# Cross-attention and FFN in one kernel: another order of scores and values, x and the FFN's weights transposed by VectorE instead of TensorE

## The chip, the cores and the metric

The kernel runs on one core of a Trainium2 chip. The time is the device time of one execution in microseconds (us). Engines are named as in the profile: PE is TensorE, PEld its weight loads, DVE VectorE, ACT ScalarE, POOL GpSimd, SP SyncE, whose queue SPq issues all transfers of this kernel.

## The reference, cut to what matters

```python
B, S, D, H, DH = 16, 64, 512, 32, 128
def xattn(hidden_q, hidden_kv, mask, position_bias, Wq, Wk, Wv, Wo):
    q = (hidden_q @ Wq).reshape(b, lq, h, dh)
    k = (hidden_kv @ Wk).reshape(b, lk, h, dh)
    v = (hidden_kv @ Wv).reshape(b, lk, h, dh)
    score = einsum('bqhd,bkhd->bhqk', q, k) * scale + position_bias      # masked keys: -inf
    probs = softmax(score, axis=-1)
    return einsum('bhqk,bkhd->bqhd', probs, v).reshape(b, lq, h * dh) @ Wo
def ffn(x, base_W, base_b, router_W, router_b, A, B, expert_map):
    base_out = einsum('btd,od->bto', x, base_W) + base_b
    probs = softmax(einsum('btd,nd->btn', x, router_W) + router_b, axis=-1)     # 15 outputs
    topk_p, topk_i = top_k(probs, 8)
    w = weights of the 8 experts, through expert_map
    h = einsum('btd,erd->bter', x, A)
    return base_out + einsum('bter,eor->bto', h * w[..., None], B) * 2.0
x = x + xattn(layernorm(x), ctx, mask, bias, Wq, Wk, Wv, Wo)
x = x + ffn(layernorm(x), ...)
```

## The kernel before, in words

There are 1024 tokens, eight tiles of 128. Every large product is done in three passes over values split into a high and a low part (`product`, six matmuls of 512 columns for one contraction of 256): ScalarE rounds to the high part, VectorE subtracts to get the low one. The projections of V, K and Q run as blocks, 16 each, in Strassen's form with seven products (`times(n, p)`, p from 1 to 7); their sums of weights are made by GpSimd (`sums_of_b`), their halves are combined by ScalarE (`copy_p1`, `copy_u`, `copy_v`, `copy_c12`) and VectorE (`make_c11`, `make_c21`, `make_c22`). V and K are stored to memory and read back by head pairs. The orders of all engines are written out by hand, each engine runs its own list, and SP's list issues the transfers in order.

While K's blocks run (n from 16 to 30), x is normalised for the attention: `moments_of_x` and `normalise` on VectorE, `rstd_of` on GpSimd, then `turn_pair(j)`, j from 4 to 7: TensorE transposes two tiles of x with eight 128 x 128 transposes in every third block, and ScalarE and VectorE split what lands in PSUM (`first_high`, `rows_out`, `last_high`, `sums_of_a`). Q's blocks need this from block 31 on.

Then come the stages of head pairs, i from 0 to 13 in the loop and the last pairs by hand. In stage i TensorE computes the scores of pair i + 1 (`scores(h + 2)`, `scores(h + 3)`), the values of pair i (`times_v(h)`, `times_v(h + 1)`), a block of Q (products 1, 2, 6, 7, then 5, 3, 4) and between those the eight tiles of pair i's Wo product (`times_wo(i, t)`). In the same stage VectorE reads the scores (`biased`), takes the maximum (`largest`), splits outputs (`o_low`) and Q's weights (`lower_of`), adds the Wo tiles to y (`add_tile(i, t)`), weights P (`weights`) and transposes it in blocks of 32 x 32 (`turn_blocks`). P goes to memory and comes back in the order that the value product wants (`store_p`, `load_p`); GpSimd adds the mask to the bias (`add_mask`). ScalarE does the exponentials in halves (`exp(h, half)`), the outputs' high parts (`o_high`) and the roundings. Its list in a stage begins `exp(h + 2, 0)`, `o_high(h, 0)`, `o_high(h, 1)`, `o_high(h + 1, 0)`, `copy_p1(n)`, `o_high(h + 1, 1)`, `exp(h + 2, 1)`, `higher_of(w, 0)`, `exp(h + 3, 0)`, `copy_u(n)`, `exp(h + 3, 1)`, `higher_of(w, 1)`; that of VectorE begins `biased(h + 2)`, `largest(h + 2)`, `biased(h + 3)`, `largest(h + 3)`, the four `o_low` with `make_c11(n)` among them, `lower_of(w, 0)`, `lower_of(w, 1)`, `add_tile(i, 0)`. `times_wo(i, t)` with t of 2 or more waits for `add_tile(i, t - 2)`, since there are two banks (pY).

SP's list in a stage: `load_k(i + 2)` once the scores are done, eight bias transfers, Wq, `load_v(i + 1)` once the values are done, in some stages the FFN's small inputs, then `store_p` and `load_p` of the two heads, then Wo.

The FFN's weights are loaded as they lie, transposed by TensorE in the last stages (`ffn_weights`, 28 transposes) and split from PSUM (`split_ffn`). At the end the second layer norm, the router and the FFN's products run tile by tile.

## Time and profile before

| | us |
|---|---|
| median of 3 runs | 779.62 (775.87 to 779.64) |
| the profiled execution | 777.37 |
| its span, first to last instruction | 775.5 |
| TensorE busy | 766.0 (99%) |
| VectorE busy | 541.8 (70%) |
| ScalarE busy | 384.8 (50%) |
| GpSimd busy | 196.6 (25%) |

The span is what lies between the first and the last instruction of the profiled execution. Busy times are sums over the span; a matmul's end is modelled, so a busy TensorE says only that nothing stopped it for long. Starts in a timeline are in us from the start of the span.

### The profile page before, as it was taken

What the parts mean: (1) busy time and instruction counts of PE and PEld (TensorE: products, weight loads), DVE (VectorE), ACT (ScalarE), POOL (GpSimd) and SP (SyncE); (2) the same over time, 40 slices, a digit from 0 to 9 for tenths busy, and PEclk for the clock granted to TensorE, in tenths of its full rate; (3) what the DMA queues carried; (4) which work ended last, traced back from release to release, by engine and by line L of the source; (5) the groups of instructions that cost most, each with busy time, mean ns of one, the idle gap of its engine ahead of it and who ended that gap; (6) DMA issues with size and microseconds to landing.
All of it is one profiled execution on the core that took longest, in us unless ns stands there. A gap on an engine that the chain in (4) does not pass through costs nothing.

```text
span 775.5 us, 16682 instructions
## 1 busy us (share of the span) xinstructions
PE 766.0 (99%) x6272; PEld 639.1 (82%) x6272; DVE 541.8 (70%) x979; ACT 384.8 (50%) x1110; POOL 196.6 (25%) x203
## 2 busy tenths in 40 slices
PE   9999999999999999999999999999999999999998
PEld 7888888888888888887888888888888888888886
DVE  5874626257677676578778877887678767867974
ACT  5662526245555464475654465435543565426510
POOL 0224041014424433323132312232122313010300
PEclk9999999999999999999999999999999999999999
DMA  6536673244565456577766777556756666541002
GB/s 231 203 123 217 220 244 137 109 140 160 163 190 164 164 163 187 167 235 217 229 181 209 226 208 208 170 176 205 201 165 197 201 188 196 154 148 57 1 15 95
DMA packets 128236, 133.05 MB, mean 172 GB/s; under 512 B 46479, under 2 KB 93583, under 8 KB 128158
## 3 DMA queue, kind: packets, MB, share of 16 engines
q1 hardware_dynamic: 128158, 132.00, 54.3%
q8 instruction: 50, 0.82, 0.4%
q14 instruction: 28, 0.23, 0.1%
HBM read 88.98 MB, written 42.99 MB: 170 GB/s over the span
## 4 chain that ended last, share of the span: by engine, by line
PE 94%; DVE 3%; issue 1%; ACT 1%; DMA 0%; ACTq 0%
PE pY L1452 43%; PE pP L1452 40%; PE pY L1613 4%; PE pO L1649 2%; PE pT_ L1649 1%; PE pO L1452 1%; DVE y L1167 1%; ACT pr L798 1%; PE pS L1649 1%; DVE st L1018 1%; PE pO L1501 0%; PE pS L1501 0%; DVE wk_lo L948 0%; PE pY L1528 0%; DVE wo_lo L948 0%
## 5 line engine op out<-in xcount | busy, mean ns | idle before, releaser
L798 ACT ACTIVATE pr<-pr,mx 128x64 f32<-128x64 f32 x256 | 86.2, 343 | 68.0 <-DVE mx L1187 68.0
L1452 PE MATMUL pY<-wo_hi,oT_hi 128*128 128x512 f32 x248 | 97.3, 392 | 0.3 <-DVE y L1167 0.2
L1452 PE MATMUL pY<-wo_lo,oT_hi 128*128 128x512 f32 x248 | 96.6, 389 | 0.0
L1452 PE MATMUL pY<-wo_hi,oT_lo 128*128 128x512 f32 x248 | 96.5, 389 | 0.0
L1167 DVE TENSOR_TENSOR y<-y,pY 128x512 f32<-128x512 f32 x124 | 83.9, 676 | 15.2 <-PE pY L1452 14.1
L690 ACT CAST wk_hi<-twk 128x256 fp32r<-128x256 f32 x128 | 50.7, 408 | 65.2 <-PE pP L1452 53.4
L948 DVE TENSOR_TENSOR wk_lo<-wk_raw,wk_hi 128x256 fp32r<-128x256 f32 x96 | 48.5, 506 | 46.5 <-ACT wk_hi L690 45.1
L1452 PE MATMUL pP<-xo_hi,wk_hi 128*128 128x512 f32 x196 | 77.9, 398 | 0.0
L1452 PE MATMUL pP<-xo_lo,wk_hi 128*128 128x512 f32 x196 | 76.4, 390 | 0.0
L1452 PE MATMUL pP<-xo_hi,wk_lo 128*128 128x512 f32 x196 | 76.4, 390 | 0.0
L623 POOL TENSOR_TENSOR bias<-bias,madd 128x512 f32<-128x512 f32 x32 | 41.3, 1306 | 137.6 <-DMA bias<-in_fside_Bx32xSxS 137.5
L948 DVE TENSOR_TENSOR wk_lo<-twk,wk_hi 128x256 fp32r<-128x256 f32 x128 | 54.5, 438 | 23.5 <-ACT wk_hi L690 23.5
L606 POOL TENSOR_TENSOR twk<-wk_raw 128x256 f32<-128x256 f32 x32 | 25.1, 784 | 168.3 <-DVE wk_lo L948 135.3
L1452 PEld LDWEIGHTS pY<-wo_hi,oT_hi 128*128 128x128 f32 x248 | 46.5, 188 | 11.7 <-DVE y L1167 1.5
L1452 PEld LDWEIGHTS pY<-wo_lo,oT_hi 128*128 128x128 f32 x248 | 46.6, 188 | 9.8
L1452 PEld LDWEIGHTS pY<-wo_hi,oT_lo 128*128 128x128 f32 x248 | 46.6, 188 | 9.3
L798 ACT ACTIVATION_READ_ACCUMULATOR pr<-pr,mx 128x1 f32 x256 | 49.5, 193 | 0.0
L1452 PE MATMUL pP<-co_hi,wk_hi 128*128 128x512 f32 x126 | 49.3, 392 | 0.0
L1452 PE MATMUL pP<-co_lo,wk_hi 128*128 128x512 f32 x126 | 49.1, 389 | 0.0
L1452 PE MATMUL pP<-co_hi,wk_lo 128*128 128x512 f32 x126 | 49.0, 389 | 0.0
L1452 PE MATMUL pY<-wv_hi,co_hi 128*128 128x512 f32 x112 | 43.8, 391 | 0.1
L1452 PE MATMUL pY<-wv_lo,co_hi 128*128 128x512 f32 x112 | 43.6, 389 | 0.0
(283 smaller groups left out, 1862.2 us busy)
## 6 DMA issues: line engine op xcount, KB each, us to landing
v_hbm<-stage SPq DMA_DIRECT2D x64, 256.0 KB, 2.1
k_hbm<-stage SPq DMA_DIRECT2D x64, 256.0 KB, 3.7
k<-k_hbm SPq DMA_DIRECT2D x16, 1024.0 KB, 6.4
v<-v_hbm SPq DMA_DIRECT2D x16, 1024.0 KB, 7.2
wk_raw<-in_L_xattn_Wk SPq DMA_DIRECT2D x16, 512.0 KB, 4.6
wo_raw<-in_L_xattn_Wo SPq DMA_DIRECT2D x16, 512.0 KB, 3.7
bias<-in_fside_Bx32xSxS SPq DMA_DIRECT2D x128, 64.0 KB, 3.6
wk_raw<-in_L_xattn_Wq SPq DMA_DIRECT2D x16, 512.0 KB, 4.6
```

The costliest lines, as they stand in the source:

```text
L606: nc.gpsimd.tensor_tensor(tw[:, 0, :, :], raw_block(w, 1, 1), raw_block(w, 0, 1), ALU.subtract).then_inc(tw_made, 1)
L623: nc.gpsimd.tensor_tensor(b[:, :, :], b[:, :, :], madd[:, :, :], ALU.add).then_inc(bias_made, 1)
L690: nc.scalar.copy(w_part(w, 0)[:, slot, :, :], w_source(w, slot)).then_inc(w_hi[slot], 1)
L798: nc.scalar.activation(pr[s][:, b, :], pr[s][:, b, :], ACT.Exp, bias=mx[:, s, b:b + 1], accum_out=sm[:, s, b:b + 1]).then_inc(exp_made, 1)
L948: nc.vector.tensor_tensor(dst, src, hi.bitcast(F32), ALU.subtract).then_inc(done, 1)
L1018: nc.vector.bn_stats(st[:, n % NX, :], y[:, t, :]).then_inc(ln_step, 1)
L1167: nc.vector.tensor_tensor(y[:, t, :], y[:, t, :], src[:, :], ALU.add).then_inc(y_added, 1)
L1452: mm = nc.tensor.matmul(bank_, a, b, start=first and n == 0, stop=last and n == len(terms) - 1, skip_group_check=read_between)
L1613: mm = nc.tensor.matmul(pY[s][64 * half:64 * half + 64, blk * S:(blk + 1) * S], q[:, s, b * S:(b + 1) * S], k[:, s, b * S:(b + 1) * S], st ...
L1649: mm = nc.tensor.matmul(o, (v if h >= 2 else v0)[rows, t, s * DH + 64 * d:s * DH + 64 * d + 64], p, start=True, stop=True)
```

## The change

Four things. (1) In the loop of head pairs TensorE's order becomes values of the first head, scores of both heads, values of the second head; in stage 0 a product of the Q block goes between. The lists of ScalarE and VectorE in the loop stay. (2) x for the attention: VectorE transposes the normalised tiles in blocks of 32 x 32 (`xb`), SP stores them and loads them back so that whole tiles come out transposed (`x_out`, `x_back`), and ScalarE and VectorE split from SBUF instead of PSUM; the steps of x begin a block earlier. (3) The FFN's weights are loaded in pieces such that a transposition of 32 x 32 blocks in place, by VectorE, gives the transposed weights; `ffn_weights` goes. The transfers of A, the router and base_W move behind Wo's load of stages 2 and 3. (4) In the last stages the order on all engines is changed, the last pair's outputs get buffers of their own (`oT_last`), pair 14's Wo products use four banks (`pQ`), and some waits are split.

```diff
+    bw_d = base_W.rearrange("(b k) (c g j) -> g k c b j", k=32, g=4, j=32)
+    a_d = A_in.rearrange("e r d -> (e r) d").rearrange("(b k) (c g j) -> g k c b j", k=32, g=4, j=32)
+    r_d = router_W.rearrange("n (c g j) -> g n c j", g=4, j=32)
+    b_d = B_in.rearrange("(g f) (b k) r -> g f k b r", f=2, k=32)
...
+            def x_out(j):
+                for i in range(2):
+                    sp.wait_ge(xb_made, 2 * j + i + 1)
+                    sp.dma_start(x_hbm[2 * j + i], xb[:, i, :, :].rearrange("p a n -> p (a n)")).then_inc(put_x[i], 16)
+            def x_back(j):
+                if j >= 1:
+                    sp.wait_ge(sum_step, 4 * (4 + j))
+                    sp.wait_ge(a01_lo, 4 + j)
+                    sp.wait_ge(a6_lo, 4 + j)
+                for i, dst in enumerate((first_x, low[1])):
+                    sp.wait_ge(put_x[i], 16 * (j + 1))
+                    blocks = x_hbm[2 * j + i].rearrange("(t k) (a n) -> a k t n", t=4, a=4)
+                    for a in range(4):
+                        sp.dma_start(dst[32 * a:32 * a + 32, :, :], blocks[a]).then_inc(ld_xt[i], 16)
...
                     load_wk(n - 10)
+                if 17 <= n < 29 and n % 3 == 2:
+                    x_out((n - 17) // 3)
                 if n != Q0:
                     store(n, 0, c11_made)
                 if 0 < n:
                     store(n - 1, 2, c21_made)
+                if 17 <= n < 29 and n % 3 == 2:
+                    x_back((n - 17) // 3)
...
-                if i == 2:
-                    sp.dma_start(a_raw[:, :], a_d).then_inc(ld_a, 16)
-                    sp.dma_start(r_raw[:, :], router_W).then_inc(ld_a, 16)
-                if i == 3:
-                    sp.dma_start(bw_raw[:, :, :], bw_d).then_inc(ld_ffn, 16)
                 if i == 4:
-                    for o in range(DC):
-                        sp.dma_start(b_raw[:, o, :].rearrange("p (e r) -> p e r", e=E), b_d[:, o]
-                                     ).then_inc(ld_ffn, 16)
+                    for g in range(4):
+                        for f in range(2):
+                            sp.dma_start(b_raw[32 * g:32 * g + 32, :].rearrange("k (b f r) -> k f b r", f=2, r=R)[:, f],
+                                         b_d[g, f]).then_inc(ld_ffn, 16)
                 h = 2 * i + 2
                 if by_blocks(h):
                     store_p(h)
                     store_p(h + 1)
                     load_p(h)
                     load_p(h + 1)
                 if i + 2 < NP:
                     sp.wait_ge(wo_l, i + 2)
                     load_wo(i + 2)
+                if i == 2:
+                    sp.wait_ge(ar_clear, 1)
+                    for g in range(4):
+                        rows = slice(32 * g, 32 * g + 32)
+                        for c in range(DC):
+                            sp.dma_start(ar_raw[rows, c, 0:ER].rearrange("k (b j) -> k b j", j=32), a_d[g][:, c]
+                                         ).then_inc(ld_a, 16)
+                        sp.dma_start(ar_raw[32 * g:32 * g + NR, :, ER:ER + 32], r_d[g]).then_inc(ld_a, 16)
+                if i == 3:
+                    for g in range(4):
+                        for c in range(DC):
+                            sp.dma_start(bw_raw[32 * g:32 * g + 32, c, :].rearrange("k (b j) -> k b j", j=32),
+                                         bw_d[g][:, c]).then_inc(ld_ffn, 16)
...
 (ScalarE, K blocks)
                     first_high(j)
-                    rows_out(j)
                     last_high(j)
...
 (VectorE, normalise)
+                for i in range(2):
+                    m = 2 * n + i
+                    dve.wait_ge(xn_made, m + 1)
+                    if n >= 1:
+                        dve.wait_ge(put_x[i], 16 * n)
+                    nc.vector.transpose(xb[:, i, :, :].rearrange("p g (c q) -> p c g q", c=DC),
+                                        xn[:, i, :].rearrange("p (c g q) -> p c g q", c=DC, g=4)).then_inc(xb_made, 1)
...
 (VectorE, loop of pairs, after add_tile(i, 7))
+                if 6 <= i < 8 + DC:
+                    dve.wait_ge(ld_a, 320)
+                    dve.wait_ge(ld_ffn, 384)
+                    raw = {6: ar_raw[:, :, :].rearrange("p c n -> p (c n)"), 7: b_raw[:, :]}.get(i)
+                    raw = bw_raw[:, i - 8, :] if raw is None else raw
+                    nc.vector.transpose(raw, raw).then_inc(fw_turned, 1)
...
 (VectorE, last stages)
+            o_low(h, 0)
+            o_low(h, 1)
             biased(h + 2)
             largest(h + 2)
-            o_low(h, 0)
-            o_low(h, 1)
             o_low(h + 1, 0)
             o_low(h + 1, 1)
             biased(h + 3)
             largest(h + 3)
-            split_ffn(0)
             add_tile(i, 0)
-            split_ffn(1)
             add_tile(i, 1)
             add_tile(i, 2)
             invert(i + 1)
             weights(h + 2)
+            weights(h + 3)
             add_tile(i, 3)
-            weights(h + 3)
+            split_ffn(0)
+            add_tile(i, 4)
+            split_ffn(1)
+            add_tile(i, 5)
+            lower_wo(NP - 1)
             split_ffn(2)
-            add_tile(i, 4)
+            add_tile(i, 6)
             split_ffn(3)
-            add_tile(i, 5)
-            add_tile(i, 6)
-            add_tile(i, 7)
-            lower_wo(NP - 1)
-            split_ffn(4)
             o_low(h + 2, 0)
             o_low(h + 2, 1)
             o_low(h + 3, 0)
             o_low(h + 3, 1)
+            add_tile(i, 7)
+            split_ffn(4)
             split_ffn(5)
-            split_ffn(6)
...
 (TensorE, K blocks)
-                if prep_at(n) is not None:
-                    turn_pair(prep_at(n))
...
 (TensorE, loop of pairs)
                 if i == 0:
                     turn_p(h)
                     turn_p(h + 1)
-                scores(h + 2)
-                scores(h + 3)
-                times_v(h)
+                    scores(h + 2)
+                    scores(h + 3)
+                    times_v(h)
+                    times(n, 2)
+                else:
+                    times_v(h)
+                    scores(h + 2)
+                    scores(h + 3)
                 times_v(h + 1)
-                for p in (1, 2, 6, 7) if i else (2, 6, 7):
+                for p in (1, 2, 6, 7) if i else (6, 7):
                     times(n, p)
...
 (TensorE, last stages)
+            times_v(h)
             scores(h + 2)
-            times_v(h)
             times_v(h + 1)
             scores(h + 3)
-            ffn_weights(0)
-            ffn_weights(1)
-            for t in range(4):
-                times_wo(i, t)
-            ffn_weights(2)
-            ffn_weights(3)
-            for t in range(4, NT):
+            for t in range(3):
+                times_wo(i, t, heads=(0,))
+            for t in range(3):
+                times_wo(i, t, heads=(1,))
+            for t in range(3, 6):
                 times_wo(i, t)
             turn_p(h + 2)
             turn_p(h + 3)
-            ffn_weights(4)
+            times_wo(i, 6)
             times_v(h + 2)
+            times_wo(i, 7)
             times_v(h + 3)
-            ffn_weights(5)
-            ffn_weights(6)
...
             pe.wait_ge(o_lo, 2 * H - 2)
-            pe.wait_ge(y_added, last_pair * NT)
             for t in range(4):
+                if t < 2:
+                    pe.wait_ge(y_added, last_pair * NT - 1 + t)
                 times_wo(last_pair, t, heads=(0,))
```

## Rows read from the trace of the kernel before

**Rows 1.** The page, busy time of each engine, its share of the span, instructions.

```profile
PE 766.0 (99%) x6272; PEld 639.1 (82%) x6272; DVE 541.8 (70%) x979; ACT 384.8 (50%) x1110; POOL 196.6 (25%) x203
```

**Rows 2.** Busy time by stretch, a K block without and one with x's transposes.

```profile
core 0: us, PE busy (x) PEld busy (x) DVE busy (x) ACT busy (x) POOL busy (x), PEclk, DMA share, GB/s
158.43:167.94 9.51, 9.51 (x43) 7.87 (x43) 5.22 (x12) 4.58 (x11) 2.32 (x3) 1.00 0.32 113
177.47:187.87 10.40, 10.40 (x51) 8.71 (x51) 6.91 (x15) 5.59 (x13) 4.82 (x6) 1.00 0.54 163
```

**Rows 3.** Busy time by stretch: pairs 1 to 13, then pairs 6 and 10.

```profile
368.84:695.48 326.64, 322.77 (x3669) 270.27 (x3670) 250.42 (x431) 164.03 (x617) 77.86 (x71) 1.00 0.65 193
494.50:519.22 24.72, 24.72 (x284) 20.68 (x286) 19.53 (x33) 12.76 (x48) 6.57 (x7) 1.00 0.60 190
595.30:619.98 24.68, 24.68 (x285) 20.74 (x286) 19.22 (x33) 12.76 (x48) 6.63 (x7) 1.00 0.66 196
```

**Rows 4.** The list of waits: us in total, times, longest.

```profile
PE pT_ L1649 <- issue: 3.9, 5, 1.0
```

**Rows 5.** Busy time by stretch, four stretches of the FFN weights' transposes, and their sum.

```profile
699.60:701.28 1.68, 1.68 (x13) 1.09 (x9) 1.68 (x4) 1.68 (x12) 0.00 (x0) 1.00 0.76 210
...
sum 4.12, PE 4.12 PEld 3.10 DVE 4.12 ACT 3.48 POOL 0.00; mean PE 1.03 PEld 0.77 DVE 1.03 ACT 0.87 POOL 0.00
```

**Rows 6.** Busy time by stretch, from the last loop stage to pair 15's Wo.

```profile
695.48:717.87 22.39, 22.29 (x404) 18.90 (x405) 18.01 (x30) 13.51 (x49) 0.00 (x0) 1.00 0.17 55
```

**Rows 7.** Timeline of PE, from values to scores: start, us, engine line op.

```profile
698.37 0.22 PE L1649 MATMUL pS<-pT,v 64*64 64x64 f32 x1
698.51 1.15 PE L1613 MATMUL pY<-k,q 128*64 128x64 f32 x32
```

**Rows 8.** Timeline of DVE in pair 6; in brackets the idle time before.

```profile
495.63 0.69 DVE L1178 SCALAR_TENSOR_TENSOR pr<-pY,bias 128x512 f32<-128x512 f32 x1 [0.40 <-PE pY L1613]
...
506.34 0.94 DVE L948 TENSOR_TENSOR wk_lo<-wk_raw,wk_hi 128x256 fp32r<-128x256 f32 x1 [3.02 <-ACT wk_hi L690]
507.20 0.67 DVE L1167 TENSOR_TENSOR y<-y,pY 128x512 f32<-128x512 f32 x1
```

**Rows 9.** Timeline of DVE in pair 10.

```profile
596.43 0.69 DVE L1178 SCALAR_TENSOR_TENSOR pr<-pY,bias 128x512 f32<-128x512 f32 x1 [0.41 <-PE pY L1613]
...
607.14 0.43 DVE L948 TENSOR_TENSOR wk_lo<-wk_raw,wk_hi 128x256 fp32r<-128x256 f32 x1 [3.02 <-ACT wk_hi L690]
607.48 0.68 DVE L1167 TENSOR_TENSOR y<-y,pY 128x512 f32<-128x512 f32 x1
...
609.77 0.71 DVE L1210 STREAM_TRANSPOSE pb<-pr 128x512 f32<-128x512 f32 x1
```

**Rows 10.** Timeline of ACT in pair 6.

```profile
497.07 0.35 ACT L798 ACTIVATE pr<-pr,mx 128x64 f32<-128x64 f32 x1 [4.87 <-DVE mx L1187]
...
500.17 0.59 ACT L663 COPY c_s<-pP 128x512 f32<-128x512 f32 x1 [0.23 <-PE pP L1452]
```

**Rows 11.** Timeline of POOL in pair 6.

```profile
505.70 1.29 POOL L623 TENSOR_TENSOR bias<-bias,madd 128x512 f32<-128x512 f32 x1 [0.52 <-DMA bias<-in_fside_Bx32xSxS]
```

**Rows 12.** Timeline of PE in pair 6, Wo's tile 2.

```profile
508.14 0.40 PE L1452 MATMUL pY<-wo_hi,oT_hi 128*128 128x512 f32 x1
```

**Rows 13.** Timeline of SP's queue in pair 4, which begins at 443.9.

```profile
445.97 0.38 SPq L449 DMA_DIRECT2D k<-k_hbm  x1
446.40 6.66 SPq L442 DMA_DIRECT2D bias<-in_fside_Bx32xSxS  x8
...
453.75 0.51 SPq L452 DMA_DIRECT2D v<-v_hbm  x1
454.30 6.90 SPq L566 DMA_DIRECT2D b_raw<-in_L_ffn_B  x4
461.25 1.48 SPq L457 DMA_DIRECT2D p_hbm<-pb  x2
```

**Rows 14.** Timeline of SP's queue in pair 10.

```profile
613.48 3.64 SPq L465 DMA_DIRECT2D pT<-p_hbm  x8
617.34 0.40 SPq L446 DMA_DIRECT2D wo_raw<-in_L_xattn_Wo  x1
```

More of the change, by code:

```diff
@@ L351, in raw_block, with first_of, second_of, like @@
             return raw[:, 2 * r:2 * r + 2, c * width:(c + 1) * width]
+        def first_of(j):
+            if j < 4:
+                return first_turn(j)[:, :].rearrange("p (c t) -> p c t", c=DC)
+            return first_x[:, :, :].rearrange("p t (c q) -> p c t q", c=DC)
+        def second_of(j):
+            if j < 4:
+                return second_turn(j)[:, :].rearrange("p (c t) -> p c t", c=DC)
+            return low[1][:, :, :].rearrange("p t (c q) -> p c t q", c=DC)
+        def like(j, a):
+            return a if j < 4 else a.rearrange("p c (t q) -> p c t q", t=4)
+        def outputs(pair):
+            return oT_last if pair == NP - 1 else oT
+        def y_tile(pair, t):
+            return {NP - 1: pL, NP - 2: pQ}.get(pair, pY + pY)[t % 4]
         def tw_of(w):
@@ L692, in first_high @@
             def first_high(j):
-                act.wait_ge(turned, FIRST_TURN[j] + 1)
-                nc.scalar.copy(a_part(j, 0)[:, 0:2, :, tile_cols(j)],
-                               first_turn(j)[:, :].rearrange("p (k c t) -> p k c t", k=2, c=2)).then_inc(a01_hi, 1)
+                if j < 4:
+                    act.wait_ge(turned, FIRST_TURN[j] + 1)
+                else:
+                    act.wait_ge(ld_xt[0], 64 * (j - 3))
+                nc.scalar.copy(like(j, a01_of(j, 0)), first_of(j)).then_inc(a01_hi, 1)
             def rows_out(j):
@@ L706, in last_high @@
             def last_high(j):
-                cols = tile_cols(j)
-                act.wait_ge(turned, SECOND_TURN[j] + 1)
-                nc.scalar.copy(a_part(j, 0)[:, 6, :, cols],
-                               second_turn(j)[:, 2 * P:4 * P].rearrange("p (c t) -> p c t", c=2)).then_inc(a6_hi, 1)
+                if j < 4:
+                    act.wait_ge(turned, SECOND_TURN[j] + 1)
+                else:
+                    act.wait_ge(ld_xt[1], 64 * (j - 3))
+                nc.scalar.copy(like(j, a_part(j, 0)[:, 6, :, tile_cols(j)]), second_of(j)[:, 2:4]).then_inc(a6_hi, 1)
             def sums_high(j):
@@ L811, in o_high @@
                 act.wait_ge(o_full, 2 * h + n + 1)
-                if s == 0 and n == 0 and i >= 1:
+                if i == NP - 1:
+                    act.wait_ge(prod, DONE[NBLK - 1, 4])
+                    act.wait_ge(s_full, H)
+                elif s == 0 and n == 0 and i >= 1:
                     act.wait_ge(y_full, NT * i)
-                nc.scalar.copy(of_parity(oT[0], s, n), pO_of[s][n][:, :].rearrange("p (t q) -> p t q", q=S)
+                nc.scalar.copy(of_parity(outputs(i)[0], s, n), pO_of[s][n][:, :].rearrange("p (t q) -> p t q", q=S)
                                ).then_inc(o_hi, 1)
@@ L904, in _ @@
             exp(h + 2, 1)
-            split_ffn(0)
             exp(h + 3, 0)
-            split_ffn(1)
             exp(h + 3, 1)
-            split_ffn(2)
-            split_ffn(3)
+            for n in range(4):
+                split_ffn(n)
             wo_high(NP - 1)
+            split_ffn(4)
             turned_p(h + 2)
             turned_p(h + 3)
-            split_ffn(4)
+            split_ffn(5)
+            split_ffn(6)
             o_high(h + 2, 0)
@@ L1165, in add_tile @@
                 dve.wait_ge(y_full, pair * NT + (t + 1))
-                src = pL[t % 4] if pair == last_pair else pY[t % 2]
+                src = y_tile(pair, t)
                 nc.vector.tensor_tensor(y[:, t, :], y[:, t, :], src[:, :], ALU.add).then_inc(y_added, 1)
@@ L1403, in _ @@
             for i in range(NT + 3):
+                if i == NT:
+                    split_ffn(6)
                 if i < NT:
@@ L1654, in times_wo @@
             def times_wo(pair, t, heads=(0, 1)):
-                if pair < last_pair:
+                if pair < last_pair - 1:
                     if t == 0:
@@ L1664, in times_wo @@
                         pe.wait_ge(y_added, pair * NT + t - 1)
-                dst = pL[t % 4] if pair == last_pair else pY[t % 2]
+                elif pair == last_pair - 1 and heads[0] == 0:
+                    if t == 0:
+                        pe.wait_ge(wo_l, pair + 1)
+                        pe.wait_ge(o_lo, 4 * pair + 2)
+                        pe.wait_ge(c12_made, NBLK)
+                        pe.wait_ge(c21_made, NBLK)
+                    if t in (2, 3):
+                        pe.wait_ge(s_read, 2 * pair + 1 + t)
+                    elif t >= 4:
+                        pe.wait_ge(y_added, pair * NT + t - 3)
+                if pair == last_pair - 1 and heads[-1] == 1 and t == 0:
+                    pe.wait_ge(o_lo, 4 * (pair + 1))
+                dst = y_tile(pair, t)
                 cols = slice(t * P, (t + 1) * P)
-                o, w = oT, wo[pair % 2]
+                o, w = outputs(pair), wo[pair % 2]
                 mm = product(dst[:, :], [((o[0][:, i, cols], o[1][:, i, cols]), (w[0][:, i, :], w[1][:, i, :]))
```

152 lines of the change are left out of this document (63 added, 89 removed).

## Prediction

> **What bounds the kernel now.** I read the page first. TensorE is busy for 766.0 of 775.5 us [rows 1] and its granted clock is full in all forty slices, so at first sight whatever leaves TensorE is won. The second view is busy time by stretch. A block of the K stage takes 9.51 us, all of it TensorE, and the same block with a turned pair of x tiles 10.40 [rows 2]. In the stage of head pairs, thirteen pairs take 326.64 us, 25.13 each; a pair that nothing disturbs takes 24.68, and TensorE idles 3.87 us in all thirteen [rows 3]. The list of waits names that idle time: five times about 1 us inside the value products, put down to "issue", so to no engine and no transfer that the profile shows [rows 4]. They fall where 128 small matmuls follow 64 others without a break. The third view, the timeline of each engine in one pair, shows how near the other engines are to deciding: VectorE is busy 19.2 to 19.5 us of a pair [rows 3], and its first addition of a Wo tile ends 0.27 us before TensorE starts the product that waits for it [rows 8, 12]. So this is a TensorE kernel with little slack behind it, and what decides is whether the new order still keeps that slack.
>
> **x through VectorE.** The change takes 32 transposes of x off TensorE: four blocks at 10.40 - 9.51 = 0.89 us [rows 2], 3.6 us gained. VectorE gets two block transposes for each pair of tiles, 0.71 us each by the like one [rows 9], 1.4 us in a block where it is busy 5.22 of 9.51 us [rows 2]; ScalarE loses a copy. SyncE issues two stores and eight loads for each pair, behind which two stores of K wait a few us; their buffers are used again two blocks, 19 us, later. The x pieces are needed first in block 31, the last come back in block 27. I cost this at nothing; without that cover it would be 1.4 us in each of four blocks, 5.7 us.
>
> **The FFN weights.** The four stretches of TensorE with their transposes sum to 4.12 us [rows 5], all of which leave. In their place VectorE has six transposes in pairs 6 to 11, 0.71 us each, behind its last addition of the pair. There it waits 0.40 us for the scores now [rows 8], and 1.15 us more by the new order (below), so they cost nothing; if the order gave no more room, 6 x 0.3 = 1.9 us.
>
> But the 4.12 us are not all won. In this part VectorE is busy 18.01 of 22.39 us [rows 6]. The new last pair starts its second Wo tile only after VectorE's addition of tile 7, which now stands behind four output splits. VectorE's list up to that point has 22 instructions of 0.69 us (eight output splits, two reads and two maxima of the scores, eight additions, two weightings), 15.2 us, and some 2.3 for four weight splits, 1.2 for Wo's and 0.45 for the reciprocals: 19.1 us, from about 1.9 us after the start, plus some 0.5 us of waiting for the exponentials and 0.5 for the last values: 21.9 to 22.1. From there seven half products of 0.68 us end at 26.8, against 27.9 now. I take -1.2 us; the bounds are -3.6 (TensorE alone decides: 4.12 less some 0.5 for switches) and 0.
>
> **Values, scores, values.** A switch of TensorE from value products to scores costs 0.14 us start to start, where value matmuls are 0.01 apart [rows 7]; the new order has one more switch in each pair. Bare TensorE time is thus 24.68 + 0.14 = 24.82. The issue stalls may go, because 128 small matmuls no longer follow the scores in one run.
>
> What the order moves is the chain behind the scores. TensorE now runs one head's values first, half of a 2.0 us stretch, and the switch: the scores come 1.15 us later in the pair. ScalarE's and VectorE's lists stay as they are: ScalarE takes the exponentials of the new scores before it rounds the outputs, and is idle for 4.87 us waiting for them [rows 10]. Behind them stand the outputs, the first product's copy, more exponentials, a weight's rounding; then VectorE's split of that weight and the addition of Wo tile 0, for which TensorE waits before tile 2. From VectorE's first read of the scores (495.63) to tile 2 on TensorE (508.14) it is 12.51 us [rows 8, 12]. In a pair where GpSimd does not overlap, read to addition is 608.16 - 596.43 = 11.73 [rows 9], with the same 0.27 to TensorE 12.00.
>
> After the change the read starts 1.13 + 1.15 = 2.28 us into the pair. ScalarE gives back the 0.23 us that it idles before the copy [rows 10]. Tile 2 so starts at 2.28 + 12.00 - 0.23 = 14.05 at best, and at 2.28 + 12.51 = 14.79 where GpSimd is in the way, against 13.85 at which TensorE could. From tile 2 to the next pair it is 519.22 - 508.14 = 11.08 [rows 3, 12]. So the period is 25.13 to 25.87, against 25.13 on average now: 0 to +8.9 us in twelve pairs. I take 25.6, because GpSimd's second mask addition follows the bias load, which follows the scores: it ends at 506.99 [rows 11], 12.49 into the pair, and would end at 13.64, while VectorE's split would start 506.34 - 494.50 + 0.92 = 12.76 in. They overlap in every pair then, and overlapped the split takes 0.94 us instead of 0.43 [rows 8, 9]. That is +5.6 us. The issue stalls lie inside this wait from then on; at worst five of them stick out by 0.45, 2.3 us. Pairs 0 and 13 get the switch and a little waiting: +0.6.
>
> The Trainium skill (SBUF — State Buffer, Who interferes with whom) says that a VectorE instruction with two SBUF inputs is blocked outright by a GpSimd instruction that reads SBUF, for that whole instruction. The trace agrees: the split ended 0.29 us after GpSimd did. By that rule alone the period is that of the later engine, about 25.6; without it 25.1.
>
> **The weights' transfers.** They go in pieces now, since VectorE transposes blocks of 32 x 32: 20 transfers for A and router instead of 2, behind pair 2's last load, 16 for base_W instead of 1 behind pair 3's, 8 for B instead of 4 ahead of pair 4's P. All are on SyncE's one queue, in order, with the next pair's k, bias, v and the way of P through memory. One such issue costs 3.64/8 = 0.46 (P) to 6.66/8 = 0.83 us (bias) [rows 13, 14].
>
> SyncE ends a pair's list 2.2 us before the pair ends (wo at 617.74, [rows 3, 14]). So base_W's 16 issues (7.3 to 13.3 us) last until 5 to 11 us into pair 4, where k is issued at 2.1 now. From k to v it is 453.75 + 0.51 - 445.97 = 8.3, B takes 6.9, and from P's store to the home-coming of the first head's last quarter (four of eight loads and about 2 us to land) some 6.5 [rows 13]. P is there 26.7 to 33 us into the pair, and the next pair now begins with it, without 2 us of scores as cover. Against 25.6 that is 1 to 7 us late. Behind A's transfers pair 3 is 0 to 4 us late (its P is made at 610.48, 15.2 into the pair [rows 9], 16.4 then). What is queued behind it is everything: values, scores and the rest of TensorE. I take +4 us; bounds 0 (it lands in time) and 11.
>
> A rule speaks against this change: the Trainium skill (DMA: Bandwidth & Descriptors, Specifications) wants 512 B or more in a piece for line rate, and base_W now comes in pieces of 128 B. By the issue times alone the stall is the above.
>
> **Sum**: -3.6 - 1.2 + 5.6 + 0.6 + 4 = +5.4 us. The profiled execution took 777.37 us (span 775.5 and 1.9 around it), so 782.8; the median of the runs shown is 779.62, 2.2 above it, so I say 784.
>
> **Rivals.** (1) It gets faster: the chain behind the scores has more slack than I read. It decides at tile 2 of each pair: where VectorE's first addition is done 13.7 us into the pair or sooner, the period is 24.82 and the loop gains 12 x 0.31 = 3.7 us instead of losing 5.6. With the end at -3.6, x at -3.6, and P in time, it is 769. For it: the stalls of [rows 4] are real and the order breaks up their run; TensorE has nothing else to wait for in [rows 3]. Against: ScalarE's list is not reordered, and 14.05 is its best by the rows. (2) No change: the chain binds as I say, but P lands in time, or the pair is nearer 25.2: -3.6 - 1.2 + 4 + 0.6, 777 to 782. For it: bounds of the issue time that reach down to no stall in pair 3 and 1 us in pair 4. (3) The pieces are slow in themselves, not only to issue: B's 4096 pieces held SyncE 6.90 us [rows 13]; base_W's 8192 at that rate take 14 us and A's 2300 another 4, so pair 4 gets P another 5 us later: 789 to 793. This is the skill's rule above, as a mechanism of this queue. For it: B's transfers, issued while v was under way, took up to three times their shortest time. Against: that may have been v.
>
> **Chances**: forecast 0.45 (781 to 788), rival 1 0.15, rival 2 0.26, rival 3 0.14. About 0.5%, 3.9 us, is what a measurement of this kernel can tell from no change. Slower by more: 0.59; within: 0.25; faster: 0.16. The range that leaves out some 2 in 10 is 774 to 793; it cuts off rival 1's core.
>
> **What would show it.** The K blocks with x take 9.5 us, as their neighbours. Pairs 1 to 12 take 25.1 to 25.9 us, TensorE waits at Wo tile 2 for VectorE's addition, and the five issue stalls are gone or inside. One long wait stands ahead of the value products of pair 5 (a shorter one at pair 4), with P's load as its end, and SyncE issues k in pair 4 at 6 us or later. The last part is about 1 us shorter, with a wait for tile 7's addition. I am wrong if pairs take 24.8 us, if no wait for P shows, or if VectorE's transposes push a K block past 9.6 us.

## The result, and the profile after

The changed kernel takes 790.96 us (median of 4 runs, 789.90 to 792.16), the kernel before 779.63 beside it: the ratio is 1.0177, 95% interval 1.0157 to 1.0196, so slower by 1.8%. The forecast was slower, 784.0, at most 793. The direction held, the size did not: +0.6% was said. (The kernel before had one run of 1092 us in that set, which the ratio leaves out; the quotient of the two medians is 1.0145, while the ratio on record fits the 776.7 to 777.4 us that the kernel before takes beside the experiments.) The profiled execution took 790.88 us, its span 789.1, 13.6 more than before.

Busy times of the page, to be read against [rows 1], and the granted clock in forty slices:

```profile
PE 768.4 (97%) x6212; PEld 635.0 (80%) x6212; DVE 551.2 (70%) x994; ACT 382.2 (48%) x1106; POOL 196.6 (25%) x203
...
PEclk9999999999999999999999998999999999999999
```

TensorE has 60 instructions fewer, yet is busy 2.4 us longer, and it idles more: 20.7 us of the span instead of 9.5. One slice has a lower clock. So some work runs slower, and there are waits. Busy time by stretch says where (columns as in [rows 2]): a K block in which VectorE now transposes x, one in which TensorE formerly did, the block that has x's last pair; pairs 1 and 2; 3; 4; 5; 6; 6 to 13; and from the last pairs to the end:

```profile
173.86:183.38 9.52, 9.52 (x43) 7.89 (x42) 6.97 (x15) 4.79 (x11) 3.37 (x5) 1.00 0.62 214
183.38:192.91 9.53, 9.53 (x44) 7.75 (x42) 7.64 (x17) 6.42 (x14) 1.71 (x3) 1.00 0.76 227
269.29:280.05 10.76, 9.79 (x43) 7.72 (x42) 7.72 (x17) 6.47 (x14) 2.60 (x4) 1.00 0.67 206
367.97:418.93 50.96, 50.57 (x566) 41.51 (x565) 39.01 (x67) 25.31 (x96) 13.11 (x13) 1.00 0.67 194
418.93:448.55 29.62, 25.46 (x283) 20.69 (x283) 21.53 (x43) 12.66 (x48) 7.29 (x7) 1.00 0.56 159
448.55:481.62 33.07, 26.97 (x282) 22.20 (x283) 19.96 (x33) 12.66 (x48) 7.08 (x6) 0.92 0.78 184
481.62:508.55 26.93, 26.93 (x282) 22.82 (x283) 18.67 (x32) 12.67 (x48) 6.03 (x6) 0.91 0.66 191
508.55:533.66 25.11, 25.11 (x283) 20.75 (x282) 18.96 (x33) 12.66 (x48) 6.64 (x7) 1.00 0.62 185
508.55:710.95 202.40, 201.27 (x2258) 166.08 (x2257) 154.90 (x263) 99.15 (x377) 45.08 (x41) 1.00 0.62 183
710.95:789.10 78.15, 73.08 (x681) 61.85 (x680) 57.87 (x151) 28.07 (x76) 6.77 (x16) 1.00 0.13 47
```

Up to pair 1 the kernel gains 0.8 us (367.97 against 368.77); thirteen pairs take 342.98 against 326.64 [rows 3], a loss of 16.3; the rest takes 78.15 against 775.5 - 695.4 = 80.1, a gain of 1.9. Pairs 3 to 5 alone take 89.62. The other ten take 50.96 + 202.40 = 253.36, 25.34 each, so the disturbance of pairs 3 to 5 costs 89.62 - 3 x 25.34 = 13.6 us, as much as the whole difference. The new order costs 13 x (25.34 - 25.13) = 2.7.

The list of PE's waits after the first 20 us:

```profile
PE pO L1738 <- DMA pT<-p_hbm: 9.4, 2, 5.5
PE pY L1551 <- DVE y L1253: 2.8, 4, 1.7
PE pS L1738 <- issue: 1.3, 3, 0.8
PE pY L1551 <- ACT u_s L738: 1.0, 1, 1.0
```

Two waits for P on its way back from memory are the bulk; from start to start they cost 4.0 us (at the end of pair 3) and 5.7 (of pair 4). The third row is the issue stalls, fewer but not gone. The longest wait for VectorE's y, 1.7, lies in the last part.

SP's queue from the end of pair 2 to that of pair 4, beside [rows 13]; pair 3 begins at 418.93, pair 4 at 448.55:

```profile
416.70 0.40 SPq L502 DMA_DIRECT2D wo_raw<-in_L_xattn_Wo  x1
417.14 1.89 SPq L638 DMA_DIRECT2D ar_raw<-in_L_ffn_A  x4
...
429.16 0.86 SPq L640 DMA_DIRECT2D ar_raw<-in_L_ffn_router_W  x1
430.07 0.55 SPq L505 DMA_DIRECT2D k<-k_hbm  x1
...
437.18 0.51 SPq L508 DMA_DIRECT2D v<-v_hbm  x1
437.73 1.25 SPq L513 DMA_DIRECT2D p_hbm<-pb  x2
445.18 3.64 SPq L521 DMA_DIRECT2D pT<-p_hbm  x8
...
449.35 10.31 SPq L644 DMA_DIRECT2D bw_raw<-in_L_ffn_base_W  x16
459.70 0.49 SPq L505 DMA_DIRECT2D k<-k_hbm  x1
...
467.30 8.21 SPq L622 DMA_DIRECT2D b_raw<-in_L_ffn_B  x8
475.56 0.96 SPq L513 DMA_DIRECT2D p_hbm<-pb  x2
478.20 3.64 SPq L521 DMA_DIRECT2D pT<-p_hbm  x8
```

SyncE issues A and the router until 430.02; pair 3's k is asked for 11.1 us into the pair instead of 2.1. The chain of waits says what came of that:

```profile
437.73 7.44 DMA p_hbm<-pb
```

P's store needed 7.44 us from its issue to P's load; in the kernel before it was 464.06 - 461.25 = 2.8 in pair 4 [rows 13] and 4.2 in pair 3. It stands behind k, eight bias transfers, Wq and v, 3072 KB by the page's sizes. The kernel before has the same 3072 KB ahead of the store in every pair; what differs is the distance to v, 0.55 us here. In the fourteen profiles together, twelve stores of P were issued 0.5 to 1.2 us behind v, and they took 7.4 to 7.8 us to land; the 380 that were issued 4.9 us or more behind v took 2.0 to 4.5. In pair 4 the store comes at 475.56, 27.0 us into the pair, behind sixteen issues of base_W (10.31 us) and eight of B (8.21): there it is the issues that last.

### The profile page after: what moved, and what is told of

Read it like the earlier page. It is cut to its first block, busy times and chain, and to the rows that moved or that the text cites. A ratio compares the mean times of both kernels' runs of the same rounds, so it can differ in the third digit from the quotient of the medians.

```text
span 789.1 us, 16665 instructions
## 1 busy us (share of the span) xinstructions
PE 768.4 (97%) x6212; PEld 635.0 (80%) x6212; DVE 551.2 (70%) x994; ACT 382.2 (48%) x1106; POOL 196.6 (25%) x203
## 4 chain that ended last, share of the span: by engine, by line
PE 79%; SPq 7%; DVE 6%; DMA 4%; ACT 2%; issue 2%; ACTq 0%; DVEq 0%
PE pY L1551 36%; PE pP L1551 35%; PE pY L1702 3%; PE pO L1738 2%; SPq L498 1%; PE pT_ L1738 1%; DMA p_hbm<-pb 1%; ACT pr L869 1%; SPq L644 1%; DVE y L1253 1%; DMA wv_raw<-in_L_xattn_Wv 1%; SPq L638 1%; SPq L622 1%; DVE wk_lo L1023 1%; PE pO L1551 1%
## 5 line engine op out<-in xcount | busy, mean ns | idle before, releaser
L1551 PE MATMUL pY<-wo_hi,oT_hi 128*128 128x512 f32 x232 | 91.6, 395 | 1.3 <-DVE y L1253 1.1
L1551 PE MATMUL pY<-wo_hi,oT_lo 128*128 128x512 f32 x232 | 90.6, 390 | 0.0
L1551 PE MATMUL pY<-wo_lo,oT_hi 128*128 128x512 f32 x232 | 90.5, 390 | 0.0
L1253 DVE TENSOR_TENSOR y<-y,pY 128x512 f32<-128x512 f32 x120 | 80.8, 673 | 12.4 <-PE pY L1551 12.4
L1023 DVE TENSOR_TENSOR wk_lo<-wk_raw,wk_hi 128x256 fp32r<-128x256 f32 x96 | 45.1, 477 | 53.1 <-ACT wk_hi L759 52.7
L1023 DVE TENSOR_TENSOR wk_lo<-twk,wk_hi 128x256 fp32r<-128x256 f32 x128 | 59.4, 477 | 20.2 <-ACT wk_hi L759 20.2
L1551 PEld LDWEIGHTS pY<-wo_hi,oT_hi 128*128 128x128 f32 x232 | 43.6, 188 | 13.9 <-DVE y L1253 4.8
L1551 PEld LDWEIGHTS pY<-wo_lo,oT_hi 128*128 128x128 f32 x232 | 43.6, 188 | 9.1
L1551 PEld LDWEIGHTS pY<-wo_hi,oT_lo 128*128 128x128 f32 x232 | 43.6, 188 | 8.5
L1551 PEld LDWEIGHTS pP<-xo_hi,wk_hi 128*128 128x128 f32 x196 | 36.8, 188 | 11.0 <-issue 3.1
```

What stands on the lines that cost most here:

```text
L1023: nc.vector.tensor_tensor(dst, src, hi.bitcast(F32), ALU.subtract).then_inc(done, 1)
L1253: nc.vector.tensor_tensor(y[:, t, :], y[:, t, :], src[:, :], ALU.add).then_inc(y_added, 1)
L1551: mm = nc.tensor.matmul(bank_, a, b, start=first and n == 0, stop=last and n == len(terms) - 1, skip_group_check=read_between)
```

## Experiments

Times are medians beside the kernel before on the same chip (776.7 to 777.4), so the ratios are what compares; the changed kernel's is 1.0177.

**e1_spread.** Behind v in SyncE's list, with the old places taken out:

```diff
+                if 2 <= i < 6:
+                    g = i - 2
...
+                    for c in range(DC):   # ar_raw, slot c, rows of g
...
+                    for f in range(2):    # b_raw, half f, rows of g
...
+                if 6 <= i < 8:
+                    for g in (2 * i - 12, 2 * i - 11):   # bw_raw, four transfers each
```

> The changed kernel, with the FFN's 44 transfers issued elsewhere: seven (five of A and the router, two of B) in each of pairs 2 to 5 and eight of base_W in pairs 6 and 7, all between v's load and P's store, where SyncE's list has some 5 us of waiting. Theory (SyncE's queue makes P late in pairs 3 and 4): both long waits go, 4.0 and 5.7 us, and the slower clock after them with 3.6 us; pairs 3 to 5 take 25.1 to 25.6 us, in all 776 to 779 us. Rival (the small pieces load the DMA engines and P comes late wherever they are issued): waits for P remain in pairs 2 to 7, 784 us or more.

779.25 us, ratio 1.0035 (1.0023 to 1.0048). Pairs 3 to 5, and the kernel from the last pairs to the end:

```profile
417.26:442.38 25.12, 25.12 (x284) 20.74 (x283) 18.96 (x33) 12.66 (x48) 6.54 (x7) 1.00 0.70 202
442.38:467.58 25.20, 25.12 (x283) 20.88 (x282) 19.90 (x42) 12.67 (x48) 6.55 (x7) 1.00 0.68 196
467.58:493.40 25.82, 25.51 (x283) 20.58 (x282) 19.78 (x33) 12.66 (x48) 6.43 (x7) 1.00 0.65 180
697.65:777.30 79.65, 74.63 (x681) 62.97 (x680) 57.88 (x151) 28.08 (x76) 6.77 (x16) 0.98 0.13 46
```

The theory holds: 11 us come back with no change of the work. The time is 0.25 us above the theory's range. What is still lost is 0.5 and 0.8 us of waiting for P at the ends of pairs 6 and 7, where base_W's eight issues behind v took 9.2 us, a stall of 2.1 us in pair 8's values, and 1.5 us in the last part: it takes 79.65 us where the changed kernel has 78.15, since the granted clock falls to 0.50 at 719.96 us, just behind the wait of 1.7 us for tile 7's addition.

**e2_wide.**

```diff
-sp.dma_start(bw_raw[32 * g:32 * g + 32, c, :].rearrange("k (b j) -> k b j", j=32), bw_d[g][:, c])
+sp.dma_start(bw_raw[32 * g:32 * g + 32, c, :], bw_w[32 * g:32 * g + 32, c, :])   # A and B alike
```

> The changed kernel with as many transfers of as many bytes at the same places, but A, base_W and B come in pieces of 512 B, 2 KB and 1 KB instead of 128, 128 and 64 B (so that A, base_W and B are not transposed and the output is another). Theory (the time that SyncE needs for each issue, some 0.45 to 1.0 us whatever the pieces, makes P late): both waits stay within 1.5 us of 4.0 and 5.7 us, 788 to 792 us in all. Rival (small pieces are slow in themselves): the waits shrink by half or more, 784 us or less.

783.88 us, ratio 1.0099 (1.0074 to 1.0123): just inside the rival's range. PE's waits in pairs 3 to 5, and two rows of SP's queue in pair 4 (from 446.14):

```profile
PE pO L1739 <- DMA pT<-p_hbm: 5.1, 2, 4.0
...
462.52 4.34 SPq L625 DMA_DIRECT2D b_raw<-in_L_ffn_B  x8
466.90 0.90 SPq L516 DMA_DIRECT2D p_hbm<-pb  x2
```

The first wait stays (4.1 us start to start), so A's cost is the number of issues, as the theory has it. The second falls from 5.7 to 1.3, with some 0.5 more for the second head: B's eight issues take 4.34 us instead of 8.21, and P's store comes 20.8 us into the pair instead of 27.0. There the rival is right, and it is the third rival of the prediction: small pieces are slow in themselves, above all where they are issued behind v, still under way. Base_W's sixteen issues, behind Wo, took 10.31 us with pieces of 128 B and 8.28 with 2 KB. (These rows are of an execution of 782.02 us with a mean granted clock of 0.998; two of the four had 0.993 and took 785.7 and 787.0, and no trace shows their waits.) The Trainium skill (DMA: Bandwidth & Descriptors, Specifications) wants 512 B or more in a piece for line rate; the rows agree for B, and for A they show no difference in the wait.

**e12_b_late.** `if i == 4:` ahead of B's transfers becomes `if i == 6:`.

> The changed kernel with B's eight transfers moved from pair 4 to the same place in pair 6. Theory (in pair 4 base_W's sixteen issues make k, bias, Wq and v as late as A's twenty did in pair 3, and P's store then queues behind v; B's eight add the rest): the wait ahead of pair 5's values shrinks from 5.7 us to that of pair 4, 3.5 to 4.5 us, and pair 7 waits for P by 0.5 us or so in its place: 787 to 790 us. Rival (B's small pieces alone hold up P in pair 4): the wait ahead of pair 5 falls to 1.5 us or less, 784 to 786 us.

786.57 us, ratio 1.0132 (1.0104 to 1.0160). The wait ahead of pair 5 is 2.9 us, some 0.5 more for the second head, and that of pair 4 stays at 4.1; none appears at pair 7. So of the 5.7 us some 2 to 3 are B's; the rest is base_W's and, with B gone, the store's, which now stands right behind v in pair 4 too:

```profile
465.94 0.51 SPq L508 DMA_DIRECT2D v<-v_hbm  x1
466.49 1.28 SPq L513 DMA_DIRECT2D p_hbm<-pb  x2
474.31 3.65 SPq L521 DMA_DIRECT2D pT<-p_hbm  x8
```

Both theories' waits were off, by 0.6 us and by 1.4 or more; the time is 0.4 below the theory's range, and behind the shorter wait the granted clock stayed at 1.00 in the profiled execution.

**e11_after_old.** The changed kernel with the old order in the loop:

```diff
-                    times_v(h)
                     scores(h + 2)
                     scores(h + 3)
+                    times_v(h)
                 times_v(h + 1)
```

> The changed kernel with one thing undone: in the loop of pairs from 1 on TensorE takes the scores of both heads first again, then the values. Theory (P comes late by SyncE's queue whatever TensorE's order, but the scores, 2.1 us, stand ahead of the values as cover): the waits for P shrink from 4.0 and 5.7 us to about 1.9 and 3.6 (0.5 us either way), the slower clock after them costs less, and pairs without a wait take 24.7 us: 780 to 784 us. Rival (the waits come back in full, because with the scores first k, bias and P of the next pair are asked for as late): 785 us or more.

785.33 us, ratio 1.0106 (1.0082 to 1.0130). The theory falls. PE's waits in pairs 4 and 5:

```profile
PE pO L1738 <- DMA pT<-p_hbm: 7.3, 2, 5.5
PE pT_ L1738 <- DMA pT<-p_hbm: 2.5, 1, 2.5
```

In pair 4 the first head's wait is shorter by 2.0 us, the scores' length, but the second head then waits 2.7 us, which the scores covered in the new order. In pair 5 it is 5.7 again. P comes back when SyncE gets to it: at 481.8 here, at 481.6 in the changed kernel. From 417 to 482 us SyncE's list, with the landing of P's stores, is the bound, and what TensorE does first there is of no account.

**e4_clock.**

```diff
+            def keep_clock(i, count):
+                pe.wait_ge(c12_made, QA + 2 + i)
+                pe.wait_ge(c21_made, QA + 2 + i)
+                for m in range(count):
+                    nc.tensor.matmul(pP[0][:, :], oT[0][:, 0, 0:P], wo[(i - 1) % 2][0][:, 0, :], start=True, stop=True)
...
+                    if i in (4, 5):
+                        keep_clock(i, {4: 16, 5: 22}[i])
                     times_v(h)
```

> The changed kernel; at the start of pairs 4 and 5, ahead of the wait for P, TensorE does 16 and 22 matmuls of 512 columns that nobody reads, 3.6 and 5.0 us, inside the waits of 4.0 and 5.7 us. Theory (after a wait of this length TensorE's granted clock is at half for 3 to 4 us, which costs 1.55 and 2.07 us in the bursts of pairs 4 and 5): the waits for P stay, the bursts take 4.2 us again, 787 to 788 us. Rival (the slow bursts come from transfers or instructions arriving late, not from the clock): the bursts stay slow and the time is 790 to 792 us.

Values and scores at the start of pairs 6, 4 and 5 of the changed kernel, by stretch:

```profile
508.55:512.75 4.20, 4.20 (x194) 4.00 (x193) 2.56 (x4) 0.46 (x3) 0.68 (x1) 1.00 0.24 89
448.55:454.29 5.74, 5.74 (x192) 5.50 (x192) 1.92 (x3) 0.51 (x3) 0.00 (x0) 0.70 0.78 173
481.62:487.90 6.28, 6.28 (x192) 6.03 (x192) 2.27 (x4) 0.89 (x5) 0.00 (x0) 0.62 0.40 118
```

and the starts of pairs 4 and 5 in e4_clock:

```profile
447.20:451.50 4.30, 4.13 (x180) 3.86 (x184) 1.98 (x3) 0.57 (x3) 0.00 (x0) 1.00 0.83 198
480.03:484.50 4.47, 3.65 (x144) 3.38 (x148) 1.55 (x3) 0.73 (x5) 0.00 (x0) 1.00 0.54 164
```

With something to do through the wait TensorE keeps its clock. Without it the same 192 matmuls take 5.74 and 6.28 us instead of 4.20, at a mean granted clock of 0.70 and 0.62; in the 4.35 us from 481.65 it is 0.50, the lower of its two levels, 1.2 of 2.4 GHz. The Trainium skill (TensorE: Matmul & The Clock Gate, What's actually happening) says that an idle TensorE is put to half its clock; the trace agrees for these two waits. But the time is 788.45 us, ratio 1.0154 (1.0138 to 1.0170), just above the theory's range; it is some 2 us less and not 3.6: what pair 4 gains its end gives back, since P comes no earlier (e11 again), and in pair 5 an issue stall of 1.0 takes half.

**e3_spread_old.** e1_spread with the old order (the edit of e11_after_old).

> The kernel with the spread transfers (e1_spread), and in the loop of pairs from 1 on TensorE's old order: scores of both heads, then values of both. Theory (in the new order TensorE waits in nearly every pair for ScalarE's copy of the first product, 0.29 us, and has one more switch of 0.14 us; the old one has only the issue stalls): an undisturbed pair takes 24.7 us again, some four or five issue stalls of about 1 us come back, the mean pair is 25.1 and the time 2 to 4 us below e1_spread, so 773 to 776 us. Rival (the new order pays for itself by taking the issue stalls away): within 1 us of e1_spread or above it.

775.26 us, ratio 0.9976 (0.9962 to 0.9990): 4.0 us below e1_spread and inside the theory's range. By the profiles not all of that is the order: 1.5 us of it is the slower clock in e1_spread's last part, which takes 78.15 us here.

**e5_even_old.** e3_spread_old, with this in place of the sixteen transfers of base_W:

```diff
+                if 6 <= i < 6 + DC:
+                    c = i - 6
+                    for g in range(4):   # bw_raw, slot c, rows of g
```

> e3_spread_old with base_W's sixteen transfers four to a pair in pairs 6 to 9 instead of eight in pairs 6 and 7. In e3_spread_old eight of them took SyncE 9.4 us (pair 7), P came 0.4 us late and pair 8 lost 4.2 us to a stall of 2.5 us inside the values and the slower clock behind it. Theory (too many issues between v and P's store make P late, and a wait or stall of over 2 us also costs clock): pairs 7 and 8 come back to 24.7 to 25.7 us, 3 to 4 us in all: 771 to 773 us where e3_spread_old had 775.3. Rival (that stall is one of the issue stalls, whose places are a matter of the instruction stream alone): pair 8 keeps 2 us or more of stall, 774 to 776 us.

771.99 us, ratio 0.9932 (0.9919 to 0.9945). Pairs 7 and 8 take 24.67 and 25.61; PE waits for P nowhere. The theory's numbers came. Whether its cause did is open: e7_even_new_p1, with the same transfers, has a stall of 2.0 us in pair 9. What the record shows is that the mean granted clock was 1.000 in all five executions here and below that in eight of e3_spread_old's twelve; the other four took 772.3 to 773.5 us, 1 us more than this kernel. The theory's "over 2 us" is no rule: in e1_spread a stall of 2.1 us left the clock at 1.00, and a wait of 1.7 us was followed by 0.50.

**e7_even_new_p1.** e5_even_old's transfers, the new order, and in ScalarE's list:

```diff
                 o_high(h, 0)
                 o_high(h, 1)
-                o_high(h + 1, 0)
                 if i:
                     copy_p1(n)
+                o_high(h + 1, 0)
                 o_high(h + 1, 1)
```

> The transfers as in e5_even_old, TensorE's new order (values, scores, values), and in ScalarE's list of a pair the copy of the first product moves up by one, ahead of the rounding of the third output. Theory (in the new order the 0.29 us inside the Q block's products is the wait for the bank that this copy empties): an undisturbed pair takes 24.82 us instead of 25.11, or up to 24.95 if Wo's tile 2 then waits; the mean pair is 24.9 to 25.1, and the time within 1 us of e5_even_old. Rival (the chain behind the scores binds at Wo's tile 2 anyway): pairs stay at 25.1, the time 2 to 4 us above e5_even_old.

775.23 us, ratio 0.9979 (0.9967 to 0.9992), 3.2 above e5_even_old. An undisturbed pair takes 25.05. TensorE no longer waits for the copy: product 6 begins 7.08 us into pair 6 instead of 7.24. But product 7 now waits for VectorE's `make_c11`, which stands behind an output split that the move made later (done at 8.41, the product begins at 8.56), and smaller delays follow. So the copy was the wait, and the next in line stood just behind it. The rival's time came, though not for its reason: at Wo's tile 2, 14.08 us in, VectorE's addition has been done for 0.4.

**e6_even_old_tail.** e5_even_old, and in VectorE's last list:

```diff
-            split_ffn(2)
             add_tile(i, 6)
-            split_ffn(3)
             o_low(h + 2, 0)
             o_low(h + 2, 1)
+            add_tile(i, 7)
             o_low(h + 3, 0)
             o_low(h + 3, 1)
-            add_tile(i, 7)
+            split_ffn(2)
+            split_ffn(3)
```

> e5_even_old, and in the last stages VectorE's addition of tile 7 stands behind two of the last output splits instead of four, and ahead of two weight splits that stood before it. Theory (TensorE's 1.9 us of idle time ahead of the last pair's second Wo tile is the wait for that addition alone, and nothing else comes late there): 1.2 to 1.9 us below e5_even_old. Rival (VectorE's list is the bound in the last stages, and what is put off is missed later): within 0.5 us of e5_even_old.

771.10 us, ratio 0.9919 (0.9906 to 0.9933), 0.9 below e5_even_old. In the profile the wait is gone and the last part takes 76.70 us instead of 78.12, 1.4 less; the medians show less than the theory's 1.2, within their spread.

**e8_x_later.** In ScalarE's K blocks `copy_u(n)` goes ahead of `last_high(j)`.

> e6_even_old_tail, and in the K blocks ScalarE rounds the second tile of x behind the copy of the sixth product instead of ahead of it. In the changed kernel TensorE idles 1.1 us in block 27 (0.7 to 0.8 in the runs since) for that copy, which stands behind a rounding that waits for x to come back from memory. Theory: the idle time goes and nothing else comes late, 0.6 to 0.9 us below e6_even_old_tail. Rival (the sums of x come late for Q's first block, or the run's own spread covers it): no difference, within 0.5 us.

770.72 us, ratio 0.9916 (0.9899 to 0.9932): no difference that can be told, and no test either, since that idle time was not in e6_even_old_tail's profile to begin with. It came in some executions, 0 to 1.1 us.

**e9_break and e10_before_break.** The break of the small matmuls (192 in a pair, with their weight loads 384 instructions), in e8_x_later and in the kernel before:

```diff
                 times_v(h)
+                if i:
+                    times(n, 1)
                 times_v(h + 1)
-                for p in (1, 2, 6, 7) if i else (2, 6, 7):
+                for p in (2, 6, 7):
```

> e8_x_later, and in the loop of pairs TensorE's run of small matmuls is broken in another way: scores of both heads, values of the first head, the Q block's first product, values of the second head; ScalarE's copy of that product moves up by one. Theory (the issue stalls come from 384 small matmuls in a row asking for instructions faster than they come, and the scores still lead the pair, so no chain is later): the stalls of 0.3 to 1.2 us in five or six pairs go, each pair pays some 0.2 us for two more switches, the mean pair 24.9 instead of 25.05: 1 to 3 us below e8_x_later. Rival (the stalls go elsewhere, or the switches eat the gain): within 1 us of e8_x_later.

> The kernel before, with this other break alone: the Q block's first product between the values of the two heads, and ScalarE's copy of it one place earlier. Theory: the five issue stalls of the kernel before, 4.9 us in all, go; thirteen pairs pay 0.2 us each; 1.5 to 3 us below the kernel before. Rival: no difference, or slower by up to 3 us, because the stalls stay and the switches come on top.

772.55 us, ratio 0.9936 (0.9920 to 0.9953), and 777.43, ratio 1.0002 (0.9993 to 1.0012). Pairs 1 to 13 of the kernel before with the break, and of e8_x_later without it:

```profile
369.27:695.27 326.00, 326.00 (x3667) 269.63 (x3666) 248.58 (x431) 163.70 (x617) 77.69 (x71) 1.00 0.65 193
...
366.27:692.21 325.94, 322.30 (x3668) 270.04 (x3667) 252.86 (x438) 163.74 (x617) 78.17 (x71) 1.00 0.67 192
```

With the break TensorE is busy for all of the 326.00 us: every issue stall of [rows 4] is gone, so they do come from the long run of small matmuls. That instructions come too slowly fits, but is not shown: in the kernel before each of the five stalls ends 1.4 to 1.5 us after a packet of the profile's instruction queue has landed. Each pair takes 25.05 to 25.11 instead of 24.68, and that eats the gain: thirteen pairs take 326.00 us against 326.64 in the kernel before [rows 3], and 325.97 in e9_break against 325.94 in e8_x_later. The rival wins in the kernel before; e9_break's median is 1.8 us above e8_x_later, outside both. In its profile, an execution of 774.5 us, 3.7 us more lie ahead of pair 1, about 3 of them in the first 13 us, where the granted clock rose at 13.1 us instead of 6.1 and no instruction differs. e8_x_later has the lowest median here, 0.8% below the kernel before and 2.6% below the changed one; e6_even_old_tail can't be told from it.

## Why the prediction was wrong

**The weights' transfers, +4 us, is the step that failed.** The mechanism was named as it happened: SyncE's one queue, pairs 3 and 4, k at 6 us or later (11.1), P as the end of the wait, and e1_spread gets it back. Its size was not: 13.6 us, beyond the bound of 11.

Three things were missing. First, the two waits were put at 0 to 4 and 1 to 7 us and then taken at 4 together; they are 4.0 and 5.7. In pair 3 the way of P from its store to TensorE took 448.55 - 437.73 = 10.8 us where the prediction has 6.5, because the store was issued right behind v. That made SyncE's list late: base_W's issues, expected 2.2 us ahead of pair 4, begin 0.8 us into it; and B's took 8.2 us where 6.9 was said. Second, TensorE falls to half clock in waits of that length, which was put at nothing: 1.5 and 2.1 us in the bursts behind them. Third, k, bias and Wq come late too, so VectorE's additions do: TensorE waits 0.5 and 0.8 us more inside pairs 3 and 4.

The measured time lies in the band of the third rival, given 0.14, and that rival was partly true at once with the forecast: by e2_wide some 6 of the 13.6 us come with the small pieces. They were not alternatives. That the scores had been cover for P, as the prediction said, does not hold here: in e11_after_old they stand ahead of the values again, and P lands as late.

**Values, scores, values: +5.6 in the loop.** The sign held; the size is 2.7 by the profile against the kernel before, and 4.0 by e1_spread against e3_spread_old, clock included. The place was wrong. Pair 6, which begins at 508.55, on ScalarE, PE, GpSimd and VectorE:

```profile
515.05 0.60 ACT L732 COPY c_s<-pP 128x512 f32<-128x512 f32 x1
...
515.40 0.39 PE L1551 MATMUL pP<-xo_lo,wk_hi 128*128 128x512 f32 x1
515.79 0.47 PE L1551 MATMUL pP<-xo_hi,wk_hi 128*128 128x512 f32 x1
...
518.80 2.54 POOL L692 TENSOR_TENSOR bias<-bias,madd 128x512 f32<-128x512 f32 x2 [9.57 <-DMA bias<-in_fside_Bx32xSxS]
...
521.23 0.43 DVE L1023 TENSOR_TENSOR wk_lo<-wk_raw,wk_hi 128x256 fp32r<-128x256 f32 x1 [3.02 <-ACT wk_hi L759]
521.57 0.68 DVE L1253 TENSOR_TENSOR y<-y,pY 128x512 f32<-128x512 f32 x1
...
522.69 0.39 PE L1551 MATMUL pY<-wo_hi,oT_hi 128*128 128x512 f32 x1
```

Undisturbed, the matmul at 515.40 is followed by the next one 0.23 us later; here it is 0.39. So 7.1 us into the pair TensorE waits for ScalarE's copy of the first product, whose bank product 6 needs (e7_even_new_p1); the chain was followed to Wo's tile 2, past a nearer consumer. At tile 2 (14.14 us in, the "at best" was 14.05) VectorE's addition has been done for 0.4 us: it ends 13.7 us in, as the first rival asked, and yet the pair does not take that rival's 24.82. (The 13.85 at which TensorE could start tile 2 does not fit the prediction's own 24.82 - 11.08 = 13.74; no term hangs on it.) GpSimd's mask additions end 12.8 us in, back to back and not at 13.6, and VectorE's split, which begins 12.7 in, takes 0.43: they hardly meet, so the 25.6 that was taken on that ground should have been the lower end, 25.13; the undisturbed pair is 25.11. Issue stalls were not gone: 0.3 to 1.0 us in pairs 1, 8, 9 and 12.

**x: -3.6.** The blocks fell from 10.40 to 9.53 as said. But block 27 took 10.76, with TensorE waiting 1.0 us for a ScalarE copy behind x's return, which was costed at nothing; pair 0 took 0.7 more, for which with pair 13 0.6 was said; and 0.65 us was lost in the first 40 us, where no changed instruction runs. So 0.8 was left at pair 1. That is one execution: in the nine other profiles with the same instructions up to there pair 1 begins at 365.90 to 367.87 us, 0.9 to 2.9 ahead of the kernel before.

**FFN weights and the last part: -1.2.** It was -1.9, inside the bounds, with the predicted wait for tile 7's addition (1.7 us). e6_even_old_tail shows that the wait was one of order, not of VectorE's load.

The sum: -0.8 + 2.7 + 13.6 - 1.9 = 13.6 us, against +5.4. The first rival failed. What left TensorE is worth 5 us all the same, as the forecast's two negative terms say, once the transfers are spread and the old order is kept (e5_even_old).

## What to carry to other kernels

Count a transfer's pieces and issues against the queue that carries them, and follow what is queued behind: 1.5 MB of weights in 44 transfers of small pieces held up every k, bias and P for 65 us. Spread over idle gaps of the queue they cost next to nothing. Ask also how close a store that others wait for comes behind a large load: right behind v, P's store took 3 to 5 us more to land. When a wait is sized, add what comes after it: the clock, and the other loads that are late by as much. And follow a delayed chain to each of its consumers in order; the first one that has no slack is the place.

## What the runs showed of the hardware that was not expected

An issue on SyncE took 0.42 to 0.55 us for A's transfers behind Wo (128 pieces of 128 B each; once 1.59), and 0.64 to 0.70 for base_W's there (512 pieces of 128 B). Right behind v it took 1.0 to 1.4 for transfers of 512 pieces of 64 or 128 B, 0.54 for the same bytes in pieces of 1 KB, and 0.56 to 0.66 for A's. P's store landed 7.4 to 7.8 us after its issue right behind v, and 2.0 to 4.5 us after it elsewhere. In the profiled executions TensorE's clock fell in or just behind waits of 4.0 to 5.7 us, one of 2.7 that followed one of 2.0 (e11_after_old), one stall of 2.5 (e3_spread_old, granted 0.50 in the products behind it) and, in e1_spread, the wait of 1.7 us in the last part; it did not behind the same wait of 1.7 in eight other profiles, nor behind waits of 1.3 and 2.9 and a stall of 2.1. So the length of a wait alone does not say what it costs. The issue stalls vanish when a product of 1.4 us stands inside the run of 192 small matmuls, in both kernels in which it was tried.
